# Attention score stacks without padding, even and odd batches in opposite halves of the partitions, and scores and shifted scores issued in turn

## What is computed

```python
def attend(q, k):                     # layer 0, causal
    s = (q @ k.T + 0.1 * (q*q) @ (k*k).T) / sqrt(8)
    return softmax(where(causal, s, -1e9)) @ V
out = 0.5 * (attend(Q, K) + attend(rotate_half(Q), rotate_half(K))) + 0.05 * (...) * gate_w
x = x + attention0(layernorm(x))      # Q, K with rotary embedding; the two attends come out equal
x = x + relu(layernorm(x) @ W1 + b1) @ W2 + b2
x = x + attention1(layernorm(x))      # softmax(q @ k.T / sqrt(8)) @ v, not causal, with biases
x = x + (silu(h @ Wg.T) * (h @ Wu.T)) @ Wd.T      # h = layernorm(x), weights from int32
```

## Time and profile before

| | |
|---|---|
| Median of 3 runs | 354.55 us (352.91 to 355.52) |
| Profiled execution | 355.51 us |
| Span of its instructions | 353.8 us |
| Mean granted TensorE clock | 0.942 of full speed |
| TensorE matmul / weight load busy | 302.2 us (85%) / 216.8 us (61%) |
| DVE / ACT / POOL busy | 252.3 (71%) / 223.8 (63%) / 168.1 us (48%) |
| Share of the chain that ended last | PE 67%, POOL 11%, DVE 9%, ACT 7%, issue 5% |

### The profile page before, as it was taken

How to read it: one execution, slowest core, us unless ns; L and a number is a source line. 1 busy time by engine, 2 the same in 40 slices (tenths; PEclk the granted TensorE clock), 3 DMA queues, 4 the chain that set the end, 5 groups by cost and what they waited for, 6 DMA issues and landing times.

```text
span 353.8 us, 8365 instructions
## 1 busy us (share of the span) xinstructions
PE 302.2 (85%) x2832; PEld 216.8 (61%) x2832; DVE 252.3 (71%) x993; ACT 223.8 (63%) x501; POOL 168.1 (48%) x383
## 2 busy tenths in 40 slices
PE   1862778597998999999999999999999999998654
PEld 1651556374675767676768676676776666665333
DVE  5776668878677777777776767679798989864422
ACT  6354266867566676767676767597777677768310
POOL 6253347756548486868685625424041403133020
PEclk9986668999899999999999999999999999999966
DMA  7667222312311112323101020020202111000000
GB/s 205 218 152 182 82 63 61 107 45 60 94 46 48 49 47 75 92 77 89 33 2 32 0 56 23 24 55 25 67 25 70 25 38 44 21 15 2 17 15 15
DMA packets 23034, 21.19 MB, mean 60 GB/s; under 512 B 2896, under 2 KB 20048, under 8 KB 22992
## 3 DMA queue, kind: packets, MB, share of 16 engines
q1 hardware_dynamic: 22992, 20.66, 21.1%
HBM read 13.18 MB, written 7.34 MB: 58 GB/s over the span
## 4 chain that ended last, share of the span: by engine, by line
PE 67%; POOL 11%; DVE 9%; ACT 7%; issue 5%; ACTq 0%; POOLq 0%
PE bank L909 14%; PE bank L883 7%; PE bank L939 5%; PE bank L830 5%; PE bank L952 4%; PE bank L866 4%; PE bank L980 4%; PE bank L988 4%; PE bank L887 4%; PE bank L867 4%; POOL RS L394 3%; PE bank L816 3%; POOL XN L401 3%; PE bank L864 2%; ACT PB L546 2%
## 5 line engine op out<-in xcount | busy, mean ns | idle before, releaser
L546 ACT ACTIVATE PB<-bank 128x384 f32<-128x384 f32 (+1 forms) x256 | 134.1, 544 | 54.7 <-PE bank L885 31.0
L711 DVE TENSOR_REDUCE NM<-bank 128x2 f32<-128x512 f32 x128 | 83.7, 683 | 25.2 <-PE bank L867 24.9
L883 PE MATMUL bank<-QS,KS 128*128 128x256 f16 x256 | 70.8, 277 | 6.0 <-ACT PB L546 5.1
L909 PE MATMUL bank<-PB,VP 128*32 128x256 f32 (+1 forms) x1024 | 61.7, 358 | 1.9 <-POOL PB L433 1.2
L706 DVE CUSTOM_DVE_ANT_0 JUNK<-bank,MSF 128x128 bf16<-128x128 f32 x128 | 36.4, 284 | 33.7 <-PE bank L864 33.6
L708 DVE CUSTOM_DVE_ANT_0 JUNK<-bank,MSF 128x256 bf16<-128x256 f32 x128 | 53.7, 420 | 0.0
L909 PEld LDWEIGHTS bank<-PB,VP 128*32 128x32 f32 x1024 | 26.7, 109 | 24.9 <-issue 10.1
L433 POOL TENSOR_SCALAR_AFFINE_SELECT PB<-PB 128x512 f32<-128x512 f32 x64 | 40.7, 636 | 0.0
L460 POOL TENSOR_TENSOR xs<-xs,Y 128x256 f32<-128x256 f32 x8 | 5.8, 727 | 66.2 <-DVE Y L720 66.2
L864 PE MATMUL bank<-KS,QS 96*128 96x256 f16 x128 | 36.1, 287 | 0.0
L883 PEld LDWEIGHTS bank<-QS,KS 128*128 128x128 f16 x256 | 24.8, 97 | 17.7 <-ACT PB L546 15.9
(11 more groups left out here) (90 smaller groups left out, 609.4 us busy)
## 6 DMA issues: line engine op xcount, KB each, us to landing
scr<-PR SPq DMA_DIRECT2D x16, 256.0 KB, 2.9
QS<-scr SPq DMA_DIRECT2D x16, 128.0 KB, 2.7
QS<-scr SPq DMA_DIRECT2D x32, 64.0 KB, 2.9
KS<-scr SPq DMA_DIRECT2D x32, 64.0 KB, 2.9
KS<-scr SPq DMA_DIRECT2D x16, 128.0 KB, 3.2
scr<-PR SPq DMA_DIRECT2D x16, 128.0 KB, 1.9
out_x<-xs SPq DMA_DIRECT2D x8, 128.0 KB, 1.8
W<-in_w SPq DMA_DIRECT2D x1, 576.0 KB, 6.0
```

Of the source, the lines that this page charges most:

```text
L546: act.activation(PB[:, s % RING, 0:n], TB_[s % 2][:, 0:n], ACT.Exp).then_inc(s_e, 1)
L711: dve.tensor_reduce(m[:, s, 0:2], o[:, :].rearrange("q (n k) -> q n k", n=2), AX.X, ALU.max, negate=True).then_inc(s_mx, 1)
L883: pe.matmul(o[:, 0:S], k[:, 0:P], q[:, :], start=True, stop=True)
L909: ins = pe.matmul(o, v, pr, start=(g % 2 == 0 and kt == 0), stop=True, skip_group_check=True)
```

## The change

The padding goes. The contraction is over as many partitions as there are rows, 48 or 24 for the scores and one more (the row of maxima and ones) for the shifted scores. A stack is no longer one of two: `QS[L]` and `KS[L]` hold the even batches from partition 0 and the odd ones from partition 64. All clears by ACT and DVE and their semaphores are dropped. POOL sets each `KS` to ones as a whole, both at the start. The number of instructions that TensorE executes stays the same, but their order and the part of the array that they use do not: in each slot the first part of the scores is followed by the first part of the shifted scores, then the second part of each.

```diff
@@
+        ROWS = [6 * HD, 3 * HD]
@@
-        QS = [[sb(f"QS{L}{p}", [P, H, S], F16) for p in range(2)] for L in range(2)]
-        KS = [[sb(f"KS{L}{p}", [P, H, S], F16) for p in range(2)] for L in range(2)]
+        QS = [sb(f"QS{L}", [P, H, S], F16) for L in range(2)]
+        KS = [sb(f"KS{L}", [P, H, S], F16) for L in range(2)]
@@ load_stack
-                h = R // 2
+                h, r0 = R // 2, P // 2 * (b % 2)
...
-                for dst, src in ((QS[L][p][0:R, cs], sq[:, cs]), (QS[L][p][R:R + h, cs], sq[0:h, cs]),
-                                 (KS[L][p][0:h, cs], sk[0:h, cs]), (KS[L][p][h:h + R, cs], sk[:, cs])):
+                for dst, src in ((QS[L][r0:r0 + R, cs], sq[:, cs]), (QS[L][r0 + R:r0 + R + h, cs], sq[0:h, cs]),
+                                 (KS[L][r0:r0 + h, cs], sk[0:h, cs]), (KS[L][r0 + h:r0 + h + R, cs], sk[:, cs])):
@@ load_max
-                sp.dma_start(QS[L][b % 2][MROW:MROW + 1, HC * c:HC * (c + 1), :], MT[i % 2][c][:, :]).then_inc(s_mi[c], 16)
+                r = P // 2 * (b % 2) + ROWS[L]
+                sp.dma_start(QS[L][r:r + 1, HC * c:HC * (c + 1), :], MT[i % 2][c][:, :]).then_inc(s_mi[c], 16)
@@ POOL, at the start
-            for p in range(2):
-
-                pool.memset(KS[0][p][MROW:P].bitcast(U32), TWO_ONES).then_inc(s_ones[0], 1)
-                pool.wait_ge(s_ones[0], p + 1)
+            for L in range(2):
+                pool.memset(KS[L][:, :, :].bitcast(U32), TWO_ONES).then_inc(s_ones[L], 1)
@@ POOL, in phase -1
-                    if i == -1 and s in (8, 13):
...
-                        pool.memset(KS[1][s // 13][MROW:P].bitcast(U32), TWO_ONES).then_inc(s_ones[1], 1)
@@ ACT
-            clear(QS[0][0][:, :, :], s_init[0][0])
-            clear(KS[0][0][0:MROW], s_init[0][0])
@@
-                    if i == -1 and s in (2, 6, 9, 12):
...
-                        clear(QS[1][n // 2][:, cs], s_init[1][n // 2])
-                    if i in (0, 1) and s in (6, 12):
-                        cs = slice(HC * (s // 12), HC * (s // 12 + 1))
-                        clear(KS[1][i][0:MROW, cs], s_init[1][i])
@@ DVE
-            dve.memset(QS[0][1][:, :].bitcast(U32), 0).then_inc(s_init[0][1], 1)
...
-            dve.memset(KS[0][1][0:MROW, 0:HC].bitcast(U32), 0)
...
-            dve.memset(KS[0][1][0:MROW, HC:H].bitcast(U32), 0).then_inc(s_init[0][1], 1)
@@ TensorE
+            def operands(i, s, rows):
+                L, b = ORDER[i]
+                half = slice(P // 2 * (b % 2), P // 2 * (b % 2) + ROWS[L] + rows)
+                return QS[L][half, s], KS[L][half, s]
+
-            def scores(i, s):
+            def scores(i, s, qt):
...
+                (q, k), o = operands(i, s, 0), SB_[g % 3]
                 if L == 0:
-                    pe.matmul(o[:, 0:P], q[:, 0:P], k[:, 0:P], start=True, stop=True)
-                    ins = pe.matmul(o[:, P:3 * P], q[:, P:2 * P], k[:, :], start=True, stop=True)
+                    if qt == 0:
+                        pe.matmul(o[:, 0:P], q[:, 0:P], k[:, 0:P], start=True, stop=True)
+                    else:
+                        pe.matmul(o[:, P:3 * P], q[:, P:2 * P], k[:, :], start=True, stop=True).then_inc(s_s, 1)
...
-            def shifted(i, s):
+            def shifted(i, s, kt):
...
+                if kt == 0:
+                    if s % HC == 0:
+                        pe.wait_ge(s_mi[s // HC], 16 * (i + 1))
+                    if g >= 2:
+                        pe.wait_ge(s_e, g - 1)
+                (q, k), o = operands(i, s, 1), TB_[s % 2]
...
@@
-                    if i + 1 < NPH:
-                        scores(i + 1, s)
-                    if 0 <= i < NPH:
-                        shifted(i, s)
+                    for part in range(2):
+                        if i + 1 < NPH:
+                            scores(i + 1, s, part)
+                        if 0 <= i < NPH:
+                            shifted(i, s, part)
```

More of the change, by code:

```diff
@@ L31 @@
 QSCALE = 1.0 / float(np.sqrt(HD))
-MROW = 96
 RING = 8
@@ L208, in program @@
         s_free = [sem(f"bank{k}_emptied") for k in range(8)]
-        s_init = [[sem(f"stacks_cleared_{L}{p}") for p in range(2)] for L in range(2)]
         s_ones = [sem("stack_ones_0"), sem("stack_ones_1")]
@@ L303, in load_stack @@
                 p, R = b % 2, NS[L] * HD
-                h = R // 2
+                h, r0 = R // 2, P // 2 * (b % 2)
                 cs = slice(HC * c, HC * (c + 1))
                 if b < 2:
-                    sp.wait_ge(s_init[L][p], 4 if L else 2)
-                    sp.wait_ge(s_ones[L], p + 1)
+                    sp.wait_ge(s_ones[L], 1)
                 else:
@@ L484, in _ @@
                                 rotate(b, n)
-                    if i == -1 and s in (8, 13):
-                        pool.wait_ge(*((s_vp, 1) if s == 8 else (s_xn[0], 3)))
-                        pool.memset(KS[1][s // 13][MROW:P].bitcast(U32), TWO_ONES).then_inc(s_ones[1], 1)
-                        pool.wait_ge(s_ones[1], s // 13 + 1)
         @block.scalar
@@ L500, in fill @@
                 return act.copy(dst, src.to_broadcast(shape))
-            def clear(t, done):
-                fill(t.rearrange("q h t -> q (h t)").bitcast(F32), 0).then_inc(done, 1)
             def copy_xt(b):
@@ L852, in _ @@
                 pe.wait_ge(s_free[k], used[k])
-            def scores(i, s):
-                (L, b), g = ORDER[i], H * i + s
-                p = b % 2
-                if s % HC == 0:
-                    pe.wait_ge(s_st[L][p][s // HC], 64 * (b // 2 + 1))
-                if g >= 3:
-                    pe.wait_ge(s_mx, g - 2)
-                q, k, o = QS[L][p][0:MROW, s], KS[L][p][0:MROW, s], SB_[g % 3]
+            def operands(i, s, rows):
[3 more added lines that the diff above has]
+            def scores(i, s, qt):
+                (L, b), g = ORDER[i], H * i + s
+                if qt == 0:
+                    if s % HC == 0:
+                        pe.wait_ge(s_st[L][b % 2][s // HC], 64 * (b // 2 + 1))
+                    if g >= 3:
+                        pe.wait_ge(s_mx, g - 2)
+                (q, k), o = operands(i, s, 0), SB_[g % 3]
                 if L == 0:
-                    pe.matmul(o[:, 0:P], q[:, 0:P], k[:, 0:P], start=True, stop=True)
-                    ins = pe.matmul(o[:, P:3 * P], q[:, P:2 * P], k[:, :], start=True, stop=True)
-                else:
-                    pe.matmul(o[:, 0:S], q[:, 0:P], k[:, :], start=True, stop=True)
-                    ins = pe.matmul(o[:, S:2 * S], q[:, P:2 * P], k[:, :], start=True, stop=True)
-                ins.then_inc(s_s, 1)
+                    if qt == 0:
+                        pe.matmul(o[:, 0:P], q[:, 0:P], k[:, 0:P], start=True, stop=True)
+                    else:
+                        pe.matmul(o[:, P:3 * P], q[:, P:2 * P], k[:, :], start=True, stop=True).then_inc(s_s, 1)
+                else:
+                    if qt == 0:
+                        pe.matmul(o[:, 0:S], q[:, 0:P], k[:, :], start=True, stop=True)
+                    else:
+                        pe.matmul(o[:, S:2 * S], q[:, P:2 * P], k[:, :], start=True, stop=True).then_inc(s_s, 1)
             def max_rows(i, c, m):
@@ L874, in max_rows @@
                 pe.transpose(m[0:HC, P:2 * P], NM[i % 2][:, cs, 1], IDF[:, :]).then_inc(*fills(f"mr{c}", i))
-            def shifted(i, s):
+            def shifted(i, s, kt):
                 (L, b), g = ORDER[i], H * i + s
-                if s % HC == 0:
-                    pe.wait_ge(s_mi[s // HC], 16 * (i + 1))
-                if g >= 2:
-                    pe.wait_ge(s_e, g - 1)
-                q, k, o = QS[L][b % 2][:, s], KS[L][b % 2][:, s], TB_[s % 2]
-                pe.matmul(o[:, 0:S], k[:, 0:P], q[:, :], start=True, stop=True)
-                if L == 0:
-                    ins = pe.matmul(o[:, S:S + P], k[:, P:2 * P], q[:, P:2 * P], start=True, stop=True)
-                else:
-                    ins = pe.matmul(o[:, S:2 * S], k[:, P:2 * P], q[:, :], start=True, stop=True)
-                ins.then_inc(s_t, 1)
+                if kt == 0:
+                    if s % HC == 0:
+                        pe.wait_ge(s_mi[s // HC], 16 * (i + 1))
+                    if g >= 2:
+                        pe.wait_ge(s_e, g - 1)
+                (q, k), o = operands(i, s, 1), TB_[s % 2]
+                if kt == 0:
+                    pe.matmul(o[:, 0:S], k[:, 0:P], q[:, :], start=True, stop=True)
+                elif L == 0:
+                    pe.matmul(o[:, S:S + P], k[:, P:2 * P], q[:, P:2 * P], start=True, stop=True).then_inc(s_t, 1)
+                else:
+                    pe.matmul(o[:, S:2 * S], k[:, P:2 * P], q[:, :], start=True, stop=True).then_inc(s_t, 1)
             def pv(i, g):
```

2 lines of the change are left out of this document (removed).

## The result

| | before | after |
|---|---|---|
| Median of the runs | 354.55 us | 380.39 us (378.56 to 384.99, 5 runs) |
| Span of the profiled execution | 353.8 us | 383.3 us |

The change takes 1.073 times as long (95% interval 1.070 to 1.077). The prediction was 346.5 us, 334 to 358 at most.

The account below looks back on a forecast made before the run. TensorE was taken to set the pace from about 90 to 330 us. Gains of 2.0 + 1.2 + 0.3 + 1.6 + 3.8, less 0.8, made 8.1 us off the 354.55 median: 346.5 us, range 334 to 358.

Parts of the forecast that it names:

- Phase 7 ... Disjoint, so I count it as the others: 0.3.: Layer 0's last shifted scores beside layer 1's first scores: overlap as in other phases, gaining 0.3 us.
- Phase 7 drains: Rival, chance 0.25: 32-row and 64-row groups can't stand side by side; phase 7 plus 5.8 us, total 352.3.
- What would show it: List of signs: right, shared starts and 0.09 us edges; wrong, among others, a low granted clock after 90 us.
- Overlap and edges, layer 0: Phases 3 to 6: slots save 1.36 plus 0.1 us, 13 switches cost 1.2; 0.3 us gained a phase.
- nothing lost: Added waits: the second score part, behind the shifted score's wait for ACT, costs no time.
- Layer 1: Phases 10 to 14: overlap less 8 switches gains 0.75 us each, 3.8 in all, with DVE not yet binding.
- Clears: Two clears on the start's chain, QS and KS, removed: gain 2.0 us; the other six lie beside other work.
- Phase 15: Only shifted scores, so no overlap and 11 switches: plus 0.8 us.
- The 47 us of overlap: Whole-kernel overlap total: 112+16 slots of 0.17 us and 112 of 0.22, set against 24.6 us of switches.
- Switches free: Rival, chance 0.16: entering part of the array costs nothing for these matmuls; about 22 us gained, 332.5.
- No overlap: Rival, chance 0.17: row groups take turns, leaving only switches of 13.5 us less 2.0 for clears; 366.
- Only the clears: Rival, chance 0.07: neither overlap nor switch cost shows; 352.5 us.

Follow-up runs that it names:

- d1: c2 with the new order in phase 7 too, its scores alternating with whole-array shifted scores; 356.6 us, ratio 1.011.
- a4: The changed kernel's new stacks in the old order, both scores and then both shifted scores; 363.7 us, ratio 1.025.
- a1: The changed kernel run again unchanged, for a second profile; 380.0 us, ratio 1.072.
- a2: The changed kernel with 64-partition halves in both layers, layer 1's new query rows cleared to zero; 360.4 us, ratio 1.015.
- b1: a2 with layer 1's row maxima taken over only the first 128 of 256 columns; 358.1 us, ratio 1.010.
- b4: a2 with a copy of 8 columns as ScalarE's first instruction, loading its table early; 358.4 us, ratio 1.015.
- c1: a3 contracted over 72 and 73 rows in place of 96 and 128, some start clears resized; 365.8 us, ratio 1.032.
- b3: a2 with even and odd batches both from partition 0, in separate stacks, so without overlap; 397.8 us (2 runs).
- c3: b4 with two more score matmuls of 256 columns ahead of each pair in phases -1 to 3; 374.2 us, ratio 1.056.
- b2: The kernel before with layer 1's row maxima taken over only the first 128 of 256 columns; 353.5 us, ratio 0.997.
- c2: Layer 0 as in the kernel before, layer 1 unpadded without its clears, new order in phases 8 to 15; 352.9 us, ratio 0.996.
- a3: The kernel before, with its padded stacks and clears on the whole array, in the new order alone; 357.6 us, ratio 1.009.

## Why the prediction was wrong, step by step

- **The step that failed: "Phase 7 ... Disjoint, so I count it as the others: 0.3."** Two sizes of part don't stand side by side. Counted: 0.3 us won. Measured: +18 to +20.6 us. The rival *Phase 7 drains* (0.25) had the mechanism and sized the changes about rightly (5.8; d1 showed 4.9), but it took the clock as given, so its 352.3 missed too. With at most 49 rows in every score, a change at each and no overlap, the clock fell to 0.53. Neither of the two alone does it: a4 has the same 24 and 49 rows with half the changes (20.9 us, full clock), d1 all the changes with 128 rows in every second matmul (23.1 us, full clock). Why the two together bring it down stays open. The Trainium skill (TensorEngine Tiling (Array Packing), Key Properties) states that a change of the mode drains TensorE; the trace agrees, with 0.10 us more from start to start at each change.
- **Not seen at all: the clock of phases 1 to 3.** +6.7 us in the profiled execution of after, 4.1 in a1 and 4.2 to 5.4 in a2, a4, b1 and b4. The last line of "What would show it" named "a low granted clock after 90 us, which no term here foresees", and that came. c1 shows that fewer contracted rows lower it there, b3 that the overlap doesn't, and c3 that a TensorE without idle time doesn't bring it back with 48 rows. The prediction took the clock of phases 1 to 3 as it was in before, and gave "a low granted clock after 90 us" no term and no chance, when it hung in part on what the matmuls contract over.
- **Overlap and edges, layer 0.** Both mechanisms were right. The edge of 0.09 us is what the rows show. But the phases 3 to 6, counted at 0.3 us each, won nothing: in a2, phases 4 to 6 took 53.0 us against 52.9. The overlap gives 1.6 a phase (counted 1.46), the edges cost 1.5 (counted 1.2, with those in the two stretches that don't follow TensorE free), and the new order another 0.16 ("nothing lost").
- **Layer 1.** 3.8 us counted in phases 10 to 14; 1.6 measured. "DVE ... doesn't bind yet" failed: it holds the chain for 8.6 us of a phase of 15.8 (a2), and with half the maxima 1.3 of the missing 2.2 us come back (b1 against b2). In those 8.6 us it works with hardly a gap, though over the whole phase it is busy 14.1 of 15.8 us: the share over a phase hid a bound inside it. The other 0.9 us these runs don't place. The prediction's 15.9 us of waiting for the exponential are those of the whole run; 7.8 of them lie in phases 10 to 15. Phases 8 and 9 won 0.95 (a2) of 1.6.
- **Clears.** 2.0 counted. The gain can't be told from the start's own scatter, and c2 leaves it open. Against it stands the table load that the clear had covered, a cost of the removal that the prediction didn't ask for: the first projections began 1.2 us later (9.05 against 7.88).
- **Phase 15**: 0.8 counted. From its first to its last shifted score it took 14.0 us in before and 14.8 in a2 and c2, so this term held.
- **A sum.** The 47 us of overlap come to 46.4 by the terms beside them; nothing in the forecast uses them.
- **The other rivals.** *Switches free* is refuted by b3 and the 0.15 us rows, *No overlap* and *Only the clears* by the shared starts at 152.42 and by b3 against a2. With one size of part and before's clock the phases from 4 on would win 1.7 us (a2 against before: +0.15, 0, -0.95, -1.6, and +0.7 for phase 15). If the table load costs its 1.2 us in full and the clears bring between nothing and 2.0, that would be some 352 to 354 us, an estimate, and no better than c2.

## What to carry to other kernels

When matmuls are moved to parts of the array, list every place where two sizes of part meet, price each change at 0.1 us, and ask what half the clock would make of the stretch; keep one size, or group the changes. A contraction cut to fewer rows takes no less time from start to start (0.06 and 0.12 us in b3, as on the whole array) and can lose the clock: between a3 and c1, rows of zeros were what kept it up. Before taking an instruction off an engine's front, ask what it covers, here ScalarE's table load; and before counting a gain on TensorE, ask how far the next engine stands behind it, in path and not in busy time.
